# Attention A's score products on two 64-column halves of TensorE, with token halves exchanged in two of four tiles

## The reference, cut to what matters

```python
q = hidden_states @ _dequant(q_codes, q_scales)      # 32 heads of 128
k = hidden_states @ _dequant(k_codes, k_scales)      # 8 key heads of 128, one for 4 query heads
...
scores = jnp.einsum('bhqd,bhkd->bhqk', q, k) * scale + mask[None, None]
attn = jax.nn.softmax(scores, axis=-1)
out = jnp.einsum('bhqk,bhkd->bhqd', attn, v)
```

## Time and profile before

| | us |
|---|---|
| median of 3 runs | 952.37 |
| lowest and highest of them | 947.94 and 952.43 |
| the profiled execution: its own time | 950.79 |
| its span, first to last instruction | 949.1 |

### The profile page before, as it was taken

How to read it: one execution, slowest core, us unless ns; L and a number is a source line. 1 busy time by engine, 2 the same in 40 slices (tenths; PEclk the granted TensorE clock), 3 DMA queues, 4 the chain that set the end, 5 groups by cost and what they waited for, 6 DMA issues and landing times.

```text
span 949.1 us, 19791 instructions
## 1 busy us (share of the span) xinstructions
PE 912.1 (96%) x6698; PEld 487.6 (51%) x6698; DVE 771.8 (81%) x1812; ACT 598.8 (63%) x1323; POOL 618.9 (65%) x668
## 2 busy tenths in 40 slices
PE   5889999999999999999999999999999989999998
PEld 3445555555555555545555555554445534444543
DVE  6888887887887788788788878898878879996764
ACT  4677666676667567666576756646463469997331
POOL 4788876968777687687777777822368744553211
PEclk9999999999999999999999999999999999999999
DMA  9177376484665556647557465464332943121145
GB/s 339 51 182 173 87 185 145 63 211 107 122 186 88 144 116 157 144 86 199 117 101 190 83 144 144 87 175 84 76 82 55 163 80 64 42 43 24 23 86 159
DMA packets 256005, 114.10 MB, mean 120 GB/s; under 512 B 244144, under 2 KB 244784, under 8 KB 251312
## 3 DMA queue, kind: packets, MB, share of 16 engines
q1 hardware_dynamic: 246416, 70.42, 39.1%
q10 hardware_dynamic: 9504, 42.49, 12.9%
HBM read 49.84 MB, written 2.10 MB: 55 GB/s over the span
## 4 chain that ended last, share of the span: by engine, by line
PE 76%; DVE 10%; ACT 6%; issue 3%; DMA 3%; POOL 1%; SPq 1%; ACTq 0%; DVEq 0%; POOLq 0%
PE bank L1253 16%; PE bank L1255 16%; PE bank L1254 16%; PE bank L1734 4%; PE bank L1352 3%; PE bank L1354 3%; PE bank L1353 3%; PE bank L1372 3%; PE bank L1374 3%; PE bank L1373 3%; ACT bank L989 2%; PE bank L1666 2%; DVE bw_hi L1981 2%; DVE bank L1964 2%; PE bank L1640 2%
## 5 line engine op out<-in xcount | busy, mean ns | idle before, releaser
L622 POOL TENSOR_TENSOR rt<-rt 128x512 f32<-128x512 f32 x80 | 101.6, 1273 | 131.8 <-DVE rt L1949 131.8
L1981 DVE SCALAR_TENSOR_TENSOR bw_hi<-bank,rden,bw_hi 128x128 f16<-128x128 f32 (+3 forms) x256 | 123.3, 544 | 60.9 <-ACT bw_hi L1025 60.9
L989 ACT ACTIVATE bank<-bank,shift,c_score 128x128 f32<-128x128 f32 (+3 forms) x256 | 147.3, 605 | 2.1
L1964 DVE CUSTOM_DVE_ANT_0 bank<-bank,mask_w 128x512 f32<-128x512 f32 (+3 forms) x256 | 117.9, 520 | 21.5 <-PE bank L1354 21.5
L1025 ACT ACTIVATE bw_hi<-bank,rden 128x128 f16<-128x128 f32 (+3 forms) x256 | 114.5, 535 | 22.4 <-DVE rden L1974 22.2
L984 ACT ACTIVATE shift<-smax,c_score 128x4 f32<-128x4 f32 x64 | 19.0, 297 | 155.4 <-DVE smax L1964 155.4
L629 POOL TENSOR_TENSOR arena<-rt,arena 128x512 f16<-128x512 f32 x80 | 92.4, 1158 | 8.6 <-ACT arena L973 7.8
L1253 PE MATMUL bank<-xt,wq_hi 128*128 128x512 f16 x256 | 97.0, 379 | 0.0
L1254 PE MATMUL bank<-xt,wq_hi 128*128 128x512 f16 x256 | 97.0, 379 | 0.0
L1255 PE MATMUL bank<-xt,wq_lo 128*128 128x512 f16 x256 | 97.0, 379 | 0.0
L1253 PE MATMUL bank<-wo_hi,arena 128*128 128x512 f16 x256 | 97.0, 379 | 0.0
(11 more groups left out here) (241 smaller groups left out, 2453.6 us busy)
## 6 DMA issues: line engine op xcount, KB each, us to landing
qcode<-in_q_codes ACTq DMA_DIRECT2D x7, 1024.0 KB, 5.0
qscale<-in_q_scales ACTq DMA_DIRECT2D x7, 1024.0 KB, 7.2
ocode<-in_o_codes ACTq DMA_DIRECT2D x7, 1024.0 KB, 4.9
oscale<-in_o_scales ACTq DMA_DIRECT2D x7, 1024.0 KB, 7.9
kvcode<-in_k_codes ACTq DMA_DIRECT2D x8, 256.0 KB, 7.5
kvcode<-in_v_codes ACTq DMA_DIRECT2D x8, 256.0 KB, 7.9
kvscale<-in_k_scales ACTq DMA_DIRECT2D x8, 256.0 KB, 8.1
kvscale<-in_v_scales ACTq DMA_DIRECT2D x8, 256.0 KB, 8.9
```

The costliest lines, as they stand in the source:

```text
L989: act.activation(a_rows(i, s), a_rows(i, s), ACT.Exp, bias=shift[:, s % 2, c:c + 1], scale=c_score[:, 0:1], accum_out=bank[3][:, SUMS_AT + ...
L1964: dve.tensor_tensor_reduce(bank[bk][:, o:o + (i + 1) * P], bank[bk][:, o:o + (i + 1) * P], mask_w[:, S - (i + 1) * P:S], 1.0, LOWEST, ALU. ...
L1981: dve.scalar_tensor_tensor(out=p_row[:, s % 2, LO_AT[i]:LO_AT[i] + P_STEP * i + 1:P_STEP], in0=turned_back(i, s), scalar=rden[:, s % 2, c: ...
```

## The change

Four things change.

1. **Scores.** Each query tile is split into two halves of 64 queries. Each half has its own 64 columns of TensorE and its own 64 PSUM partitions, and only as many keys stream past it as its last query uses: (i x 128) + 64 for the earlier half, (i + 1) x 128 for the later one. The three terms of both halves are issued by turns. The matmul on columns 0 to 63 is always issued first.
2. **Exchanged halves.** In query tiles 0 and 1 (`SWAPPED`) the later 64 queries go to columns 0 to 63 and the earlier 64 to columns 64 to 127. So in these tiles of `x` the two halves of the tokens are exchanged all the way: the host lays the input out so, the transposes for attention A and B put the tokens back in order as they write (an output of two pieces in place of one), those of B's output exchange them again, and the output leaves in two DMAs of 64 tokens for each tile (line 585 of the new code), all 8 tiles alike. A second mask, `back_w`, is loaded and converted for the exchanged tiles.
3. **Leftovers.** Where a half's keys end 64 early, PSUM keeps what was there. The mask adds -1e30 to it. In the very first set 4 matmuls of zeros clear each of the two banks of tiles 0 and 1.
4. **Counts.** A half signals for itself, so DVE's waits count 6 to a set in place of 3. They are for the same points as before.

```diff
 A_ORDER = (3, 0, 2, 1)
+SWAPPED = (0, 1)
...
+        def in_order(a, t):
+            return a.rearrange("p (f n) -> p f n", f=2)[:, ::-1] if t % ST in SWAPPED else a
...
+            sp.dma_start(back_f, t_in["mask_back"]).then_inc(d_const, 16)
             sp.dma_start(x[:, ST:NT, :], x_in[:, ST:NT, :]).then_inc(d_x[ST], 16)
...
-                sp.dma_start(o_out[:, t, :], x[:, t, :]).then_inc(d_out, 16)
-            sp.wait_ge(d_out, 16 * NT)
+                for f in range(2):
+                    r = (1 - f if t % ST in SWAPPED else f) * P // 2
+                    sp.dma_start(o_out[f * P // 2:(f + 1) * P // 2, t, :], x[r:r + P // 2, t, :]).then_inc(d_out, 16)
+            sp.wait_ge(d_out, 2 * 16 * NT)
...
-                    mm = pe.transpose(bank[LN_BANK[c][t]][:, k * P:(k + 1) * P],
+                    mm = pe.transpose(in_order(bank[LN_BANK[c][t]][:, k * P:(k + 1) * P], t),
...
-                    o_ap = bank[bk][:, o:o + w]
-                    qs = slice(i * P, (i + 1) * P)
-                    pe.matmul(o_ap, q_hi[:, s, qs], k_hi[:, b, 0:w], start=True, stop=False)
-                    pe.matmul(o_ap, q_hi[:, s, qs], k_lo[:, b, 0:w], start=False, stop=False)
-                    mm = pe.matmul(o_ap, q_lo[:, s, qs], k_hi[:, b, 0:w], start=False, stop=True)
-                    if i != 0:
-                        mm.then_inc(s_ps, 1)
+                    if first and s == 0 and i in SWAPPED:
+                        for c0 in range(0, S, P):
+                            pe.matmul(bank[bk][:, c0:c0 + P], mask_w[:, 0:P], mask_w[:, 0:P], start=True, stop=True)
+                    halves = [(i * P + f * P // 2, (1 - f if i in SWAPPED else f) * P // 2, i * P + (f + 1) * P // 2)
+                              for f in ((1, 0) if i in SWAPPED else (0, 1))]
+                    terms = ((q_hi, k_hi), (q_hi, k_lo), (q_lo, k_hi))
+                    for k, (qa, ka) in enumerate(terms):
+                        for q0, r0, keys in halves:
+                            mm = pe.matmul(bank[bk][r0:r0 + P // 2, o:o + keys], qa[:, s, q0:q0 + P // 2],
+                                           ka[:, b, 0:keys], start=(k == 0), stop=(k == len(terms) - 1))
+                            if i != 0 and k == len(terms) - 1:
+                                mm.then_inc(s_ps, 1)
...
-                        dve.wait_ge(s_ps, 3 * n + {3: 1, 0: 2, 1: 3}[i])
+                        dve.wait_ge(s_ps, 6 * n + {3: 2, 0: 4, 1: 6}[i])
                     dve.nop(nofuse=True)
+                    mask = back_w[:, (1 - i) * P:2 * P] if i in SWAPPED else mask_w[:, S - (i + 1) * P:S]
...
+            dve.tensor_copy(back_w[:, P:2 * P], back_f[:])
```

More of the change, by code:

```diff
@@ L230, in build @@
         ident = sb("ident", [P, P], F32)
-        mask_f = sb("mask_f", [P, P], F32)
         mask_w = sb("mask_w", [P, S], BF16)
         mask_b = mask_w[:, S - P:S]
+        back_w = sb("back_w", [P, 2 * P], BF16)
         cos_b = sb("cos_b", [P, ST, B_HD // 2], F32)
@@ L310, in build @@
         scn = arena[:, 0:sum(QUANT_COLS.values())]
+        mask_f, back_f = arena[:, 4096:4096 + P], arena[:, 4096 + P:4096 + 2 * P]
         q_hi = arena[:, 0:2048].bitcast(F16).rearrange("p (s n) -> p s n", s=8)
@@ L465, in build @@
         block = ctx.enter_context(nc.Block())
-        N_CONST = 3
+        N_CONST = 4
         @block.sync
@@ L586, in _ @@
             pool.memset(mask_w[:, 0:S - P], 0.0).then_inc(consts, 1)
+            pool.memset(back_w[:, 0:P], 0.0).then_inc(consts, 1)
             pool.wait_ge(consts, 4)
@@ L1543, in turn @@
                 for k in range(KT):
-                    mm = pe.transpose(bk[:, k * P:(k + 1) * P], src[:, k * P:(k + 1) * P], ident[:])
+                    mm = pe.transpose(in_order(bk[:, k * P:(k + 1) * P], m), src[:, k * P:(k + 1) * P], ident[:])
                 mm.then_inc(mt_ps, 1)
@@ L1961, in a_max @@
                     if i != 2:
-                        dve.wait_ge(s_ps, 3 * n + {3: 1, 0: 2, 1: 3}[i])
+                        dve.wait_ge(s_ps, 6 * n + {3: 2, 0: 4, 1: 6}[i])
                     dve.nop(nofuse=True)
+                    mask = back_w[:, (1 - i) * P:2 * P] if i in SWAPPED else mask_w[:, S - (i + 1) * P:S]
                     dve.tensor_tensor_reduce(bank[bk][:, o:o + (i + 1) * P], bank[bk][:, o:o + (i + 1) * P],
-                                             mask_w[:, S - (i + 1) * P:S], 1.0, LOWEST, ALU.add, ALU.max,
+                                             mask, 1.0, LOWEST, ALU.add, ALU.max,
                                              smax[:, s % 2, c:c + 1]).then_inc(smax_done, 1)
@@ L2427, in constants @@
     sel = np.tile(half, (2, 1)).astype(np.float32)
-    return {"ident": np.eye(P, dtype=np.float32), "mask": mask, "cos_a": cos_a.astype(np.float32),
+    return {"ident": np.eye(P, dtype=np.float32), "mask": mask, "mask_back": np.concatenate([mask[P // 2:], mask[:P // 2]]), "cos_a": cos_a.astype(np.float32),
             "sin_a": sin_a.astype(np.float32), "cos_b": table(np.cos(phase)), "sin_b": sin_b, "sel": sel}
@@ L2442, in even_odd, with by_halves @@
         return w.reshape(-1, heads, A_HD // 2, 2).swapaxes(2, 3).reshape(w.shape)
+    def by_halves(v):
+        v = v.reshape(B, ST, 2, P // 2, D).copy()
+        for t in SWAPPED:
+            v[:, t] = v[:, t, ::-1]
+        return v.reshape(B, S, D)
     def by_group(w):
@@ L2456 @@
     arrays = {
-        "x": a[pre + "hidden_states"], "scales": np.concatenate(scales, axis=1),
+        "x": by_halves(a[pre + "hidden_states"]), "scales": np.concatenate(scales, axis=1),
         "q_codes": by_group(q), "k_codes": by_group(k), "v_codes": by_group(a[pre + "v_codes"]),
```

## The result

| | before | changed |
|---|---|---|
| median, us | 952.4 (20 runs, 947.9 to 955.8) | 955.3 (20 runs, 951.8 to 958.3) |
| ratio, 95% interval | | 1.0027 [1.0016, 1.0038] |
| the profiled execution, us | 950.8 | 955.55 |
| its span, us | 949.1 | 953.8 |

The change makes the kernel slower by 2.6 us [1.5 to 3.6] by the ratio (the medians differ by 2.9). That is less than the 0.5% within which I had counted a time as no change. The two profiled executions are 4.8 us apart. The forecast was 7.8 for that pair.

The account below looks back on a forecast made before the run. TensorE was taken to bound the kernel, without a gap in attention A. Sets +7.0, first set +0.5, zeros +0.4, queues +0.1, output +0.3 and returned waits -0.5 made +7.8 us: 960 us as a median, range 951 to 972.

Parts of the forecast that it names:

- TensorE bounds attention A and nothing hides a longer set: Attention A: TensorE has no gap, so 0.11 us more in each of 64 sets adds 7.0 us.
- 0.10 us for each switch, and first weights exposed, 0.24 together: Edges of each score set: column mode costs 0.10 us each way, plus first weights not loaded ahead; 0.24 us a set.
- The halves' 3520 keys: Score sets: matmuls starting in program order make a set last 3520 keys, 1.50 us, 0.13 less than before.
- the lower bound, +5.1: Score sets: with free halves of 3456 keys a set saves 0.16 us against 0.24 of switching, +5.1 us in all.
- Weights of 64 columns cost nothing in tile 0: Tile 0 of each set: two 64-column weight loads take 0.055 us, just what streams, so 0 was added.
- The two slower rivals: Score sets: pairs wait for their longer half, 968.6 us, chance 0.19; weight loads bind in tile 0, 970.8 us, chance 0.12.
- Waits that come back, -0.5, and zeros inside four sets, +0.4: Five sets waiting for DVE give back 0.11 us each, -0.5; two more switches in each of four sets, half hidden, +0.4.
- Zeros in the first set, +0.5: First set: zeros ahead of tiles 0 and 1 and four more switches, 0.84 us, of which 0.5 was taken.
- Output, +0.3: Kernel end: the last tile has two DMA issues in a row, +0.3 us, bounds 0 and 0.6.
- From the profiled execution to the median, +1.6: Whole kernel: the earlier median lay 1.6 us above its profiled execution, so 958.6 became 960 us as a median.
- 0.1 for the mask: First 26 us: one more load on SP, one DVE copy and one POOL memset, 0.1 us, at most 0.7.
- The chance of 0.76 for slower by over 0.5%: Whole kernel: chance 0.76 of slower, against 0.13 for within 0.5% (947.6 to 957.1 us) and 0.11 for faster.

Follow-up runs that it names:

- e5: Kernel before with one full-array product of 172 columns of zeros (0.074 us) ahead of each set; 954.1 us, ratio 1.0039 to the kernel before.
- e3: Changed kernel with a full-array product of 8 columns of zeros inside each set, four mode switches in place of two; 966.8 us, ratio 1.0179 to before.
- e4: Kernel before with a full-array product of 8 columns of zeros ahead of tile 2 in each set, no switch; 951.9 us, ratio 1.0013.
- e10: Kernel before with only the second mask's load, copy and memset added, the mask unused; 950.3 us, ratio 0.9998 to the kernel before.
- a0: Changed kernel timed once more, unaltered, against the kernel before; 954.9 us, ratio 1.0053.
- e2: Changed kernel with each pair issued the other way round, columns 64 to 127 first; 954.9 us, ratio 1.0043 to the kernel before.
- e7: Changed kernel with query tiles that are not exchanged leaving in one output DMA each; 954.0 us, ratio 1.0019 to the kernel before.
- e8: Changed kernel with four column parts of 32 queries instead of two of 64, for time alone; 969.7 us, ratio 1.0186 to the kernel before.

## Why the prediction was right and wrong

The forecast, 960.0, was 4.7 us too high, with the right sign and inside its range. The steps:

1. *TensorE bounds attention A and nothing hides a longer set*: right for the sets that do not wait. e5's padding came out, 0.075 x 53 = 3.98 against 3.3 on the stretch: the five waiting sets give back 0.16 each, and sets 24 and 40 take 0.2 more together.
2. *0.10 us for each switch, and first weights exposed, 0.24 together*: right. 0.093 in and 0.10 out in the changed kernel, 0.235 with all that goes with them; 0.205 for a pair by e3 less e4. This was the term that decides the sign, and it was read from two places of attention B.
3. *The halves' 3520 keys*: **this is the step that failed.** "Matmuls start in program order, however" was carried over from full-array products, where no row can show otherwise. The records show starts out of program order, so a half is 3456 keys and the set +0.075, not +0.11. Of these 0.035 us the 64 keys are 0.027 and rounded terms the rest; 64 x 0.035 = 2.2 us less. I had this case as the lower bound, +5.1; measured, 64 x 0.075 = 4.8.
4. *Weights of 64 columns cost nothing in tile 0*: right. 128-key matmuls stay 0.056 us apart. The two slower rivals (0.19 and 0.12) both fell.
5. *Waits that come back, -0.5, and zeros inside four sets, +0.4*: **the second that failed.** The five sets are as forecast, 5 x 0.11. But sets 1, 4, 62 and 63, where the zeros stand, are not 0.4 us longer: they take 5.30, 5.24, 3.86 and 4.99 us against 5.44, 5.51, 4.12 and 5.03 before, since TensorE waits there anyway (in sets 1 and 4 0.37 us less each). All 63 sets after the first with what stands between them cost 3.37 us, where 63 x 0.075 = 4.73 had to be expected: 1.36 come back, not 0.1.
6. *Zeros in the first set, +0.5*: undersized. From its first score matmul to the next full product this set takes 2.58 us, a usual one of the changed kernel 1.60; so the zeros cost 0.98 and hid behind nothing. The way into column mode does not show there: from the last transpose to the first score matmul it is 0.24 us in both kernels. In all the first set is 0.94 longer (2.815 us against 1.871). Another 0.7 had come about before it, as a longer wait for ACT (2.16 against 1.41, in the rows of the first set above). e4 and e5, which have no second mask, begin the first set 1.2 and 2.2 us later than the kernel before, so 0.7 is within what single executions scatter there; e10 excludes a cost of the mask above 1.0 us.
7. *Output, +0.3*: undersized; 0.85 by the ends of thirteen kernels. I priced the second issue (0.33) and not that each half takes longer to issue (0.47 and 0.60) than the whole.
8. *From the profiled execution to the median, +1.6*: this failed too. The changed kernel's profiled execution, 955.55, lies 0.2 above its median, so the shift of the one execution of before was carried over to a kernel that it has nothing to do with. In that pair the miss is 3.05 us (958.6 against 955.55), in the medians 4.7. This step moves the forecast time and not the +7.8.

So the parts that the change makes come to 0.94 (first set) + 3.37 (the others) + 0.85 (output) = 5.2 us by the traces, where the forecast had 7.8: some 2.2 too much for the sets' keys and roundings, 1.3 for waits, 0.1 for the mask, and 0.9 too little for the first set and the output. By the traces of a0 the same parts are 4.8. The two spans differ by 4.76: 5.2, the 0.7 before the first set, and 1.1 less in the rest after attention A. That rest takes 301.4 us in the changed kernel with its longer output end and 301.6 before, and between 298.8 and 303.1 in all thirteen traces. The kernel before had two half-rate stretches of the clock there, this execution of the changed one had one, near 700; that would account for up to 1.7 us.

Whole kernels measured +5.0 (a0), +4.1 (e2) and +2.6 (the first comparison), and e7, whose parts are 5.2 less 0.85, +1.8 [0.5 to 3.2]. The intervals of the first two hold what the parts give, those of the other two end over 1 us below it; these two are the comparisons in which the kernel before had its highest medians (952.4 and 951.1). Why is open. So the sign and the size of each set's cost are shown, and the size for the whole kernel only as 2.6 to 5 us.

The chance of 0.76 for slower by over 0.5% was too high: on my own numbers the lower bound of the main term, with nothing lost at the ends, was 955, within 0.5%. I gave it a fifth of the forecast because a rule with no row behind it held the keys at 3520.

## What to carry to other kernels

Splitting a product by columns pays only if the keys or columns saved in one stay in column mode are worth more than the way in and out: 0.205 us by e3 less e4, 0.235 by the set itself, which at 0.417 ns is 490 to 560 streamed columns of fp16; here 384 were saved in each set. Put more column-mode work between one way in and one way out, and balance the parts' sums, not the pairs: parts need no balance term by term. A DMA that is last in the kernel should be one DMA over all partitions; and a shift between one profiled execution and a median belongs to that execution, not to the forecast.

## What the runs showed of the hardware that I had not expected

- Column parts of TensorE take their next matmul each on its own. With two parts of unequal length, the second 128-key matmul of one part started at 307.20, before the first 64-key matmul of the other at 307.23, which stands ahead of it in the program. By these starts one signal from the last matmul would not tell that the other part is done; in this kernel each half signals, and no run tries it otherwise.
- A DMA of 64 partitions takes longer to issue than one of 128 with twice the bytes: 0.47 and 0.60 us against 0.33 at the end of the kernel.
- The way in and out of column mode is 0.10 us each, whether 0.76 or 1.5 us of streaming lie between.
- The granted clock falls to half rate for some 3.4 us near 14, 35, 700 and 780 us in some executions of a kernel and not in others: the kernel before had three of these, the changed kernel one, the changed kernel again none before its end. In e8 it was at half rate also after waits of 8.9, 3.7 and 3.9 us.
